# Gated delta rule: the output gate's products leave the block of projections and stand where the inversion had idle products

## The reference, cut to what matters

```python
q = short_conv(x @ Wq, conv_wq)     # 6 heads of 32
k = short_conv(x @ Wk, conv_wk)     # 6 heads of 32
v = short_conv(x @ Wv, conv_wv)     # 6 heads of 64
beta = sigmoid(x @ Wb)              # 6 columns
g = -exp(A_log) * softplus(x @ Wa + dt_bias)   # 6 columns
o = gated_delta_rule(q, k, v, g, beta)
gate = x @ Wg                       # 384 columns
o = o * rsqrt(mean(o * o) + EPS) * norm_weight
o = o * silu(gate)
return o @ Wo
```

## Time and profile before

| | us |
|---|---|
| median of 3 runs | 1444.47 |
| lowest, highest | 1443.03, 1448.0 |
| the profiled execution | 1452.11 |
| its span, from first to last instruction | 1450.6 |
| block of projections in it | 326.9 to 369.8 |
| block of the inversion in it | 419.0 to 486.8 |

### The profile page before, as it was taken

One profiled execution on the slowest core, in us unless ns is written; L12 is line 12 of the kernel. 1 busy time (PEld: TensorE's weight loads), 2 busy tenths in 40 slices (PEclk: granted clock), 3 DMA queues, 4 the chain that ended last, 5 costly groups with the idle time before them and its releaser, 6 DMA issues. The chain is left out here.

```text
span 1450.6 us, 32890 instructions
## 1 busy us (share of the span) xinstructions
PE 1356.5 (94%) x13699; PEld 738.5 (51%) x13707; DVE 896.1 (62%) x2147; ACT 693.5 (48%) x1037; POOL 278.1 (19%) x343
## 2 busy tenths in 40 slices
PE   7999998999679988999999979999899999988999
PEld 3355554475345774654555544445355555554436
DVE  3799994766585456749999645333655556425431
ACT  5487787646473225546777832111544444442110
POOL 4322513001320000043000000111433434200110
PEclk9999999999889999999999999999999999999999
DMA  3323300100300000022222030002200000000000
GB/s 86 68 40 64 64 14 1 34 1 2 117 1 4 16 1 16 1 58 39 35 36 34 2 115 0 1 0 38 32 13 19 13 16 13 7 1 1 1 0 29
DMA packets 33957, 37.47 MB, mean 26 GB/s; under 512 B 9153, under 2 KB 24626, under 8 KB 33810
## 3 DMA queue, kind: packets, MB, share of 16 engines
q1 hardware_dynamic: 33810, 35.39, 11.3%
HBM read 18.43 MB, written 1.07 MB: 13 GB/s over the span
## 5 line engine op out<-in xcount | busy, mean ns | idle before, releaser
L616 DVE TENSOR_REDUCE row_max_pieces<-psum 128x1 f32<-128x512 f32 (+3 forms) x672 | 407.2, 647 | 116.1 <-PE psum L510 113.6
L717 ACT ACTIVATE probs<-psum 128x1024 f32<-128x1024 f32 (+7 forms) x384 | 343.7, 900 | 212.6 <-PE psum L510 212.2
L564 PE MATMUL psum<-probs,v_ones 128*32 128x256 f32 (+1 forms) x2688 | 239.0, 376 | 9.0 <-POOL probs L499 4.6
L510 PE MATMUL psum<-q_all,k_head 97*32 97x512 f32 (+3 forms) x1536 | 190.7, 488 | 0.0
L510 PE MATMUL psum<-k_stack,q_stack 96*32 96x512 bf16 x2048 | 159.7, 380 | 3.5 <-DMA k_stack<-arena 1.3
L510 PE MATMUL psum<-q_stack,k_stack 97*32 97x512 bf16 x2048 | 158.0, 379 | 0.0
L564 PEld LDWEIGHTS psum<-probs,v_ones 128*32 128x32 f32 x2688 | 88.3, 109 | 85.5 <-POOL probs L499 22.2
L510 PE MATMUL psum<-k_head_bf,q_all_bf 80*32 80x512 bf16 (+3 forms) x768 | 93.6, 331 | 2.3 <-ACT k_head_bf L2487 1.1
L510 PEld LDWEIGHTS psum<-k_stack,q_stack 96*32 96x32 bf16 x2048 | 57.0, 95 | 72.4 <-DVE row_max_pieces L616 19.7
L510 PEld LDWEIGHTS psum<-q_all,k_head 97*32 97x32 f32 x1536 | 78.9, 109 | 29.3 <-issue 3.9
L2129 PE MATMUL psum<-xn_features,arena 128*128 128x512 f32 (+1 forms) x192 | 84.1, 621 | 0.0
(11 more groups left out here) (368 smaller groups left out, 2083.2 us busy)
## 6 DMA issues: line engine op xcount, KB each, us to landing
q_stack<-arena SPq DMA_DIRECT2D x32, 96.0 KB, 2.7
k_stack<-arena SPq DMA_DIRECT2D x32, 96.0 KB, 2.6
arena<-gd_g_sums SPq DMA_DIRECT2D x6, 512.0 KB, 6.1
q_stack<-arena SPq DMA_DIRECT2D x32, 64.0 KB, 2.3
k_stack<-arena SPq DMA_DIRECT2D x32, 64.0 KB, 2.3
x_tokens<-in_x SPq DMA_DIRECT2D x4, 256.0 KB, 3.7
k_stack<-arena SPq DMA_DIRECT2D x32, 32.0 KB, 2.3
q_stack<-arena SPq DMA_DIRECT2D x32, 32.0 KB, 2.1
```

The costliest lines, as they stand in the source:

```text
L510: last = pe.matmul(o[j:j + 32], by[:, j:j + 32], rows, **flags)
L564: last = pe.matmul(psum[32 * g:32 * g + VW, PVB, a - g * D:D], V[:, c, h, :], pr[:, n % PB, a:(g + 1) * D], start=(c == 0), stop=(c == (2 ...
L616: last = dve.reduce_max(mx[:, h % 2, qt, i:i + 1], o[:, 0:plain], AX.X)
L717: act.activation(pr[:, n % PB, q_from(c):], psum[:, 2 * (n % 2):2 * (n % 2) + 2, :].rearrange("p a n -> p (a n)")[:, q_from(c):], ACT.Exp, ...
```

## The change

The gate's products leave the first block. What stays there is a product of 12 columns for each tile of tokens (`decay_and_beta`), all eight in a row behind the second `project`, into one bank, and copied by VectorE with one instruction. The gate's columns of the weights are loaded a second time, into `w_gate`, which is the memory of the last two tiles of `SG` (they are written last). In the inversion, `gate(t, k)` is one product of 384 columns over half of the features; two of them make a tile. They stand where the 16 `keep_busy` stood. ScalarE's silu (`keep_gate`) and GpSimd's multiplication by `norm_weight` come with them; the silus of tiles 6 and 7 both wait for the last product, since their outputs overwrite the weights.

```diff
+        w_gate = SG[:, NT - KT:, :]
...
                     def loads(sp):
+                        for k in range(KT):
+                            sp.dma_start(w_gate[:, k, :], d["wgab"][k * P:(k + 1) * P, 0:VWD]).then_inc(gate_loaded, 16)
                         sp.dma_start(nw[:], ...
...
-                            pool.wait_ge(nw_loaded, 16)
-                            for t in range(NT):
-                                pool.wait_ge(gate_out, t + 1)
-                                gated = SG[:, t].rearrange("p (h c) -> p h c", c=GV)
-                                pool.tensor_tensor(gated, gated, nw[:].unsqueeze(1).broadcast_to([P, GH, GV]), ALU.mult)
...
-                            def gates(t):
-                                if t >= 2:
-                                    pe.wait_ge(gate_out, t - 1)
-                                    pe.wait_ge(ab_out, t - 1)
+                            def decay_and_beta(t):
                                 for k in range(KT):
-                                    last = pe.matmul(psum[:, 6 + t % 2, 0:VWD + 2 * GH], XNT[:, k, t * P:(t + 1) * P],
-                                                     wgab[:, k, :], start=(k == 0), stop=(k == KT - 1))
-                                last.then_inc(gate_in, 1)
+                                    last = pe.matmul(psum[:, 6, t * 2 * GH:(t + 1) * 2 * GH], XNT[:, k, t * P:(t + 1) * P],
+                                                     wgab[:, k, VWD:], start=(k == 0), stop=(k == KT - 1))
+                                last.then_inc(ab_in, 1)
...
-                                for t in GATES[f]:
-                                    gates(t)
+                                if f == 1:
+                                    for t in range(NT):
+                                        decay_and_beta(t)
...
-                                for t in GATES[f]:
-                                    keep_ab(t)
+                                if f == 1:
+                                    dve.wait_ge(ab_in, NT)
+                                    dve.tensor_copy(AB[:].rearrange("p t n -> p (t n)"), psum[:, 6, 0:NT * 2 * GH])
...
+                        def gate(t, k):
+
+                            if k == 0 and t >= 2:
+                                pe.wait_ge(gate_out, t - 1)
+                            last = pe.matmul(psum[:, 6 + t % 2, 0:VWD], XNT[:, k, t * P:(t + 1) * P], w_gate[:, k, :],
+                                             start=(k == 0), stop=(k == KT - 1))
+                            if k == KT - 1:
+                                last.then_inc(gate_in, 1)
+
+                        def x16(b, t):
...
                                 if i == CB // 2 - 1:
-                                    keep_busy(pe, 6, 1)
+                                    gate(t, 0)
                             last.then_inc(x16_in, 1)
-
-                        def y16(b):
+                            gate(t, 1)
...
-                        for stage in (x16, y16):
-                            for b in range(2):
-                                stage(b)
-                                keep_busy(pe, 6, 1)
+                        for b in range(2):
+                            x16(b, b)
+                        for b in range(2):
+                            y16(b, 2 + b)
                         for b in range(2):
                             x32(b)
-                            keep_busy(pe, 6, 1)
-                        x16(2)
-                        keep_busy(pe, 6, 1)
+                            gate(4, b)
+                        x16(2, 5)
                         y32(0)
-                        keep_busy(pe, 6, 1)
-                        y16(2)
-                        keep_busy(pe, 6, 1)
+                        gate(6, 0)
+                        y16(2, 7)
                         y32(1)
-                        keep_busy(pe, 6, 1)
+                        gate(6, 1)
...
+                        def keep_gate(t):
+                            act.wait_ge(gate_in, t + 1 if t < NT - KT else NT)
+                            act.activation(SG[:, t, :], psum[:, 6 + t % 2, 0:VWD], ACT.Silu).then_inc(gate_out, 1)
+
                         for b in range(2):
                             keep_x16(act, b)
+                            keep_gate(b)
+                        for b in range(2):
+                            keep_gate(2 + b)
                         for b in range(2):
                             act.wait_ge(t32_done, b + 1)
                             place_rows(act.activation, b, **copy)
                             keep_x32(b)
+                        keep_gate(4)
                         keep_x16(act, 2)
+                        keep_gate(5)
                         for b in range(2):
                             act.wait_ge(y_in, b + 1)
                             join(act.activation, b, **copy)
+                        keep_gate(6)
+                        keep_gate(7)
                         act.wait_ge(t32_done, 3)
                         place_rows(act.activation, 2, **copy)
```

More of the change, by code:

```diff
@@ L1210, in _ @@
                             sp.wait_ge(head_loads, 32)
+                            sp.wait_ge(gate_loaded, 16 * KT)
                         @block.gpsimd
@@ L1267, in _ @@
                         def _(act):
-                            def gate(t):
-                                act.wait_ge(gate_in, t + 1)
-                                act.activation(SG[:, t, :], psum[:, 6 + t % 2, 0:VWD], ACT.Silu).then_inc(gate_out, 1)
                             act.wait_ge(loaded, 16 * 5)
@@ L1281, in _ @@
                                                    ACT.Copy, scale=cw[:, f, TAPS - 1:TAPS]).then_inc(tapped, 1)
-                                for t in GATES[f]:
-                                    gate(t)
                                 if f >= 1:
@@ L1321, in _ @@
                                                              ALU.mult, ALU.add).then_inc(conv, 1)
-                                for t in GATES[f]:
-                                    keep_ab(t)
+                                if f == 1:
+                                    dve.wait_ge(ab_in, NT)
+                                    dve.tensor_copy(AB[:].rearrange("p t n -> p (t n)"), psum[:, 6, 0:NT * 2 * GH])
                                 if 1 <= f <= NQK:
                                     sum_squares(f - 1)
-                            for t in GATES[NF]:
-                                keep_ab(t)
                 with ExitStack() as tmp3:
@@ L1653, in w_features @@
                             last.then_inc(w_in, 1)
-                        def x16(b):
+                        def gate(t, k):
[6 more added lines that the diff above has]
+                        def x16(b, t):
                             pe.wait_ge(t_turned[slot_of(b * CB)[0]], 1)
@@ L1661, in x16, with y16 @@
                                 if i == CB // 2 - 1:
-                                    keep_busy(pe, 6, 1)
+                                    gate(t, 0)
                             last.then_inc(x16_in, 1)
-                        def y16(b):
+                            gate(t, 1)
+                        def y16(b, t):
                             pe.wait_ge(t_turned[slot_of(b * CB)[0]], 2)
@@ L1763, in _ @@
                         y32(2)
+                        pe.wait_ge(gate_out, NT)
                         keep_busy(pe, 7, 1)
@@ L1782, in _ @@
                         keep_busy(pe, 0, kept_busy // 2)
+                    @block.gpsimd
+                    def _(pool):
+                        for t in range(NT):
+                            pool.wait_ge(gate_out, t + 1)
+                            gated = SG[:, t].rearrange("p (h c) -> p h c", c=GV)
+                            pool.tensor_tensor(gated, gated, nw[:].unsqueeze(1).broadcast_to([P, GH, GV]), ALU.mult)
                     @block.scalar
```

9 lines of the change are left out of this document (2 added, 7 removed).

## The result

| | before | after |
|---|---|---|
| median, us | 1445.93 (20 runs) | 1452.07 (20 runs) |
| lowest, highest | 1442.1, 1455.15 | 1444.68, 1468.89 |
| after to before | | 1.0045, interval 1.0026 to 1.0065 |
| profiled execution, its span | 1452.11, 1450.6 | 1445.13, 1443.4 |
| mean granted clock in it | 0.980 | 0.982 |

The change makes the kernel slower, by 6.5 us on the ratio (0.0045 x 1446). The forecast was a gain of 2.4 us, too small to count as a change (1442.1, at most 1446.5), so it was wrong in direction, and the time lies outside its range. The ratio leaves out the three executions of after that lie more than 1.5% above its fastest.

What follows compares the result with a forecast made beforehand. Bounds: a 6.05 us VectorE-ScalarE ring in the projections, TensorE and VectorE in turn in the inversion. Terms -0.1 - 1.4 - 1.3 + 0.4 = -2.4 us take the median from 1444.5 to 1442.1 us, range 1439.3 to 1446.5.

Steps and rivals of the forecast that it cites:

- the term for the fillers: Inversion: 384-column products replacing 512-column fillers shorten TensorE's work, -1.4 us up to y16(0) and -1.3 us from x16(2) to x64(0).
- its slower rival: TensorE from x16(1): clock stays low; a few us longer 1443.5 to 1447, chance 0.10; long 1449 to 1456, chance 0.08.
- The term up to y16(0): Inversion: five shorter fillers between x16(0) and the end of y16(0) save 1.4 us, bounds 1.0 and 2.1.
- Cost 0: Projections: the row of 32 12-column instructions takes 4 us of TensorE but costs nothing, hidden by slack.
- The same in the projections would cost nothing to 5 us: Projections: a clock staying low there would cost nothing to 5 us; 355 to 361 ran that pattern at 1.00.
- The ring: Projections: VectorE's taps, ScalarE's silu and ScalarE's first tap form a closed period of 6.05 us, unchanged without gate products.
- The last turn, cold: End of the projections: wholly at the lower clock TensorE's last turn takes 2.1 us, twice 1.04.
- the decays at 42.6 to 43.2 us: Sign: the decays begin 42.6 to 43.2 us behind the start of the projections' block; before, 42.9.
- The table load: ScalarE: the 1.28 us silu table loads, before the projections' first silu and in an inversion wait, hide and cost 0.
- TensorE's wait behind x64(0): Inversion: two silus delay ScalarE, so TensorE's wait grows from 0.17 to 0.6 us; a term of +0.4 us.
- GpSimd against VectorE: Rival, substitution behind y16(0): one GpSimd product stops VectorE for 0.98 us, giving 1443.1; chance 0.25.
- the other seven fall into waits or transpositions: Inversion: GpSimd's products other than tile 2's do not hold up VectorE, being a good 2 us apart.

Runs made afterwards that it cites:

- x_proj: The changed kernel plus two unread products of 396 columns for each gate tile that had stood behind f = 2 to 6 in the projections: 1455.58 us, ratio 1.0047.
- w_spread: The changed kernel with only its 12-column products spread over the feature tiles, an unread 384-column product behind each tile's; inversion as changed: 1450.69 us, ratio 1.0023.
- Experiment 4: The kernel before with only the 16 fillers of the inversion shortened from 512 to 384 columns: 1453.68 us, ratio 1.0041.
- x_short: The kernel of Experiment 4: the kernel before with its 16 inversion fillers at 384 columns: 1453.68 us, ratio 1.0041.
- experiment 10: The kernel x_late with its 12-column products spread over the feature tiles, an unread 384-column product behind each tile's, VectorE's copy moved: 1444.47 us, ratio 0.9985.
- y_proj: The changed kernel's projections alone: 512-column fillers replace the inversion's gate products, no gate silus, GpSimd writes ones: 1444.66 us, ratio 0.9978.
- (11): The kernel of experiment 10 plus a 512-column filler ahead of x16(2), run twice: 1443.12 us, ratio 0.9981, and 1443.34 us, ratio 0.9987.
- Experiment 7: The changed kernel with inversion places back at 512 columns, GpSimd's products after all silus, silus 6 and 7 later: 1447.72 us, 1.0002; again 1450.06 us, 1.0017.
- x_late: The kernel of Experiment 7: 512 columns at each inversion place, GpSimd's products and two silus late: 1447.72 us, 1.0002; second run 1450.06 us, 1.0017.
- x_wait: The changed kernel with inversion places back at 512 columns, plus a 512-column filler ahead of x16(2): 1448.99 us, ratio 1.0015.

## Why the prediction was wrong

**The step that failed** is the term for the fillers, -1.4 us up to y16(0) and -1.3 us from x16(2). It priced a filler's 128 columns as time of TensorE only. Without them the clock stayed low. From x16(2) to x64(0) TensorE took 11.2 us in before's profile, so 9.9 were forecast; the two profiles of the changed kernel have 12.9 (450.54 to 463.41 in the first), and 17.0 and 17.1 where the clock stayed low (x_proj, w_spread). The prediction knew this as its slower rival, with the right place (x16(1) on) and chances of 0.10 and 0.08. Its price, +9 us if low until x64(0), gives 1453.6 and the median measured is 1452.07; that these are so near is in part luck, since the price is for one execution and the median is of executions with short and with long dips. Experiment 4 shows that rival alone: from x16(2) to x64(0) 17.1 us, and low for 10 us beyond x64(0)'s start. What was mis-sized is how often it comes: 8 of 12 executions there and 18 of 26 of the changed kernel are at 1450 us or above, against 25 of 124 of before, enough to move the median into 1449 to 1456, which was given 0.08. The term up to y16(0) met the same thing: from x16(0) to x16(2) x_short took 27.5 us where before's profile has 22.9, while the profile of after has 19.8, since no dip fell there. The argument that made it small was "narrow stages with one filler of 512 per 1.7 us held 1.00 in 446 to 456, and the gate's share is not far from it". That row shows that the clock held with 512 and says nothing of 384, and the row next to it, 0.51 with TensorE 5.00 of 5.00 us busy, showed that this block could lose the clock already. A pattern that has lost the clock once in the same trace can't be costed at nothing when it is thinned.

**A second step failed.** "What comes is 32 instructions of 12 columns in a row ... Cost 0" was right for their own time (4.04 us, 4 predicted) and wrong for what they do: the clock falls behind them in some executions, and the next `project` takes 5.5 to 5.7 us in place of 3.6. "The same in the projections would cost nothing to 5 us" held the size (the block grew by 2.7 us), but the comparison with 355 to 361 was with another pattern, one turn and one project, without the row. How much of the median this costs is not settled. The pools give 4.9 us to the edit of experiment 10, the profiles give 1.6 of it to the block, and y_proj has the same row with 1 of its 12 executions at 1450 us or above, but without the gate's silus and GpSimd's products. Experiment 10 also moved VectorE's copy and added products, which wasn't taken apart.

**The base** was 1.5 us too low: the sum starts from a median of 3 runs, 1444.47, where 20 runs give 1445.93.

**What was right.** The ring: 6.05 us predicted, 6.04 measured, so the gates were not in the way. The last turn, cold, 2.1 us predicted, 1.97 measured; the decays at 42.6 to 43.2 us, 43.06 measured (45.6 in after's second profile, with the dip). The table load hides. TensorE's wait behind x64(0): 0.6 predicted, 0.76 measured; with the two silus moved (11) it is 0.18. That term was right and is 0.6 us of 6. GpSimd against VectorE: the rival priced one product, 0.98 us; measured are 0.67 us in each of two substitution operations (0.91 - 0.24, and 0.97 - 0.29 = 0.68), of which the second stands behind y16(0), where VectorE is the bound. So that rival's mechanism was there as well, with two thirds of its price. "SBUF — State Buffer", section "Who interferes with whom", in the Trainium skill says such pairs exclude each other; the rows agree for this form: both long operations end within 0.2 us of the end of GpSimd's product (436.42 and 436.33, 443.28 and 443.12). That "the other seven fall into waits or transpositions" was not so: one product stands beside the substitution ahead of y16(0) and the last two beside the four copies of 465.39; VectorE waited behind both, 2.35 and 1.66 us, so in this execution they cost nothing. Experiment 7 could not tell the time of all this from nothing.

**What the prediction's signs would have said.** VectorE's wait for y16(0) was 2.35 us (5.4 predicted), since in that execution the stretch ran at full clock. TensorE's wait ahead of x16(2) was 1.12 us (1.5, or 0.5 with GpSimd in the way). The inversion's block was 0.9 us shorter than in before's profile (67.7 and 66.8), just inside the 0.8 to 3.5 that were to confirm the forecast. Read alone they call for a gain, and that they came out so is luck of the two executions profiled. The sign that mattered, the clock from 443 to 466, was below 1.00 (0.91 and 0.79), where the earlier trace rows had 1.00 in 446 to 456.

**What stays open.** Whether the clock falls in the projections, and how long it stays low in the inversion, differs from execution to execution of one program; the runs give how often, not why in this one. In all 7 profiles with a low stretch from x16(0) on, a wait of TensorE of 0.7 to 1.4 us ends within 2.5 us of its start; but waits as long (1.07 us in x_late, 1.12 in x_wait) stand in profiles without one. And how the 6.5 us divide between the inversion, the projections and the layers behind them is not known: the pools give shares to edits, not to places.

## What to carry to other kernels

A product whose result nobody reads may be holding the clock: before real work takes its place, compare the columns, not only the place; here, giving each place its 512 columns back took more than half of the loss away. When TensorE's clock is part of the question, judge by many executions with their mean clocks; one profile shows which way it can go wrong, and may be the exception. Before a difference between two profiles is put down to a change, see how much of it lies in blocks that the change doesn't touch. Where small products are gathered into a row for neatness, look at what follows them on TensorE, since that is what may run slowly.

## What the runs showed of the hardware

- Among 16- and 32-column products, with fillers of 512 columns the one low stretch in 11 profiles lasted 6.8 us; with 384 columns the clock stayed at 0.50 for 51.2 us in one profile (x_short, 435 to 486) and for 6.8 to 30.7 us in four others, with 256 for 41.0 us. In x_short TensorE had no idle time in 443 to 486: being busy all the time did not bring the clock back there.
- 32 instructions of 12 columns (4.0 us, back to back) were followed by 0.50 for 3.4 to 6.8 us in 5 of 9 profiles.
- Mean granted clock goes with most of the spread between executions: 9.7 us per 0.01 over 169 executions (correlation -0.94), and 24 us in 1450 between the executions of after alone.
- GpSimd's 128x384 product and VectorE's product or sum of two SBUF operands: 0.91 us where 0.24 is usual, and 0.97 where 0.29 is, in the two cases shown.
